# Router logits by another route: reads through (read weights times centred gate), in a fused memory-and-experts kernel, with routing 4 steps behind instead of 5

## What is computed

```python
x = x + attn(layernorm(x))       # out32 + (alpha * reads) @ W_read.T : a decaying memory, 4 heads of 64
x = x + ffn(layernorm(x))        # top 2 of 8 experts
# ffn:
logits = einsum('bsd,ed->bse', x, gate_w)
probs = softmax(logits); topk_probs, topk_idx = top_k(probs, 2)
h = gelu(x @ w1[e].T + b1[e]);  y = h @ w2[e].T + b2[e]
out = sum(y * topk_probs)
```

## Time and profile before

| | us |
|---|---|
| median of 3 timed runs | 559.88 (559.78, 559.88, 563.1) |
| the profiled execution | 562.67 |
| its span, first to last instruction | 560.9 |
| PE busy | 530.1 (95%) |
| DVE busy | 448.4 (80%) |
| ACT busy | 338.3 (60%) |
| POOL busy | 246.9 (44%) |

### The profile page before, as it was taken

How to read it: one execution, slowest core, us unless ns; L and a number is a source line. 1 busy time by engine, 2 the same in 40 slices (tenths; PEclk the granted TensorE clock), 3 DMA queues, 4 the chain that set the end, 5 groups by cost and what they waited for, 6 DMA issues and landing times.

```text
span 560.9 us, 17645 instructions
## 1 busy us (share of the span) xinstructions
PE 530.1 (95%) x5234; PEld 415.3 (74%) x5234; DVE 448.4 (80%) x1375; ACT 338.3 (60%) x856; POOL 246.9 (44%) x291
## 2 busy tenths in 40 slices
PE   7799899999999999999999999999999999999991
PEld 7677778778786777777777777777777777777770
DVE  4889999999987689868768787688777777778861
ACT  6899989898745876445545554455544544545540
POOL 5625778888746084523223233223322333322433
PEclk9999999999998999999999999999999999999997
DMA  5576867777345396433263364343344454344323
GB/s 161 201 229 225 258 185 234 210 222 231 126 105 129 87 216 101 71 60 62 51 103 56 53 105 77 63 68 61 61 63 79 78 78 75 68 64 67 63 37 36
DMA packets 85096, 63.33 MB, mean 113 GB/s; under 512 B 54224, under 2 KB 77392, under 8 KB 85008
## 3 DMA queue, kind: packets, MB, share of 16 engines
q1 hardware_dynamic: 71328, 43.94, 32.3%
q0 software_dynamic: 13392, 18.27, 17.3%
q10 hardware_dynamic: 288, 0.00, 0.0%
HBM read 37.56 MB, written 24.62 MB: 111 GB/s over the span
## 4 chain that ended last, share of the span: by engine, by line
PE 77%; DVE 10%; issue 4%; DMA 3%; ACT 2%; POOL 1%; SPq 1%; POOLq 0%; DVEq 0%; ACTq 0%
PE psum L1697 32%; PE psum L1712 21%; PE psum L1714 10%; PE psum L1509 3%; DVE weights L874 2%; PE psum L1592 2%; PE psum L1573 2%; PE psum L1599 2%; PE psum L1520 2%; DVE arena L1052 1%; PE psum L1559 1%; DMA arena<-sent_rows 1%; PE psum L1612 1%; PE psum L1496 1%; DVE arena L1063 1%
## 5 line engine op out<-in xcount | busy, mean ns | idle before, releaser
L1697 PE MATMUL psum<-arena,weights 128*128 128x256 f16 (+1 forms) x2208 | 279.7, 249 | 1.1 <-DVE arena L1316 1.0
L1697 PEld LDWEIGHTS psum<-arena,weights 128*128 x2208 | 187.4, 98 | 79.3 <-issue 4.1
L589 POOL DMA_INDIRECT out<-arena,tile_in x71 | 115.0, 1619 | 233.4 <-DVE arena L1343 126.9
L1712 PE MATMUL psum<-weights,arena 128*128 x556 | 211.7, 381 | 0.0
L826 ACT ACTIVATE arena<-psum,b_cur 128x256 f32<-128x256 f32 (+1 forms) x368 | 131.4, 423 | 129.9 <-PE psum L1697 115.6
L1714 PE MATMUL psum<-weights,arena 128*128 x556 | 152.0, 273 | 0.0
L1327 DVE TENSOR_TENSOR arena<-arena 128x512 f16<-128x512 f32 x142 | 98.5, 694 | 10.8 <-ACT arena L843 6.3
L559 POOL DMA_INDIRECT sent_rows<-arena,tiny x64 | 65.4, 1022 | 35.5 <-issue 17.8
L1323 DVE CAST arena<-arena 128x512 f16<-128x512 f32 x126 | 53.5, 424 | 8.8 <-ACT arena L826 8.5
L1712 PEld LDWEIGHTS psum<-weights,arena 128*128 128x128 f16 x556 | 54.4, 98 | 5.0
L1714 PEld LDWEIGHTS psum<-weights,arena 128*128 128x128 f16 x556 | 54.5, 98 | 4.6
(11 more groups left out here) (199 smaller groups left out, 642.9 us busy)
## 6 DMA issues: line engine op xcount, KB each, us to landing
weights<-in_experts SPq DMA_DIRECT2D x32, 512.0 KB, 4.8
arena<-sent_rows SPq DMA_DIRECT2D x100, 64.0 KB
arena<-in_b SPq DMA_DIRECT2D x46, 128.0 KB, 3.2
arena<-in_x SPq DMA_DIRECT2D x16, 256.0 KB, 3.4
out<-arena SPq DMA_DIRECT2D x16, 256.0 KB, 4.1
arena<-sent_rows SPq DMA_DIRECT2D x84, 32.0 KB
sent_rows<-pad SPq DMA_DIRECT2D x7, 265.0 KB, 4.6
tile_in<-sent_rows SPq DMA_DIRECT2D x71, 4.5 KB, 2.6
```

The lines of the kernel that those rows point to most:

```text
L589: pool.indirect_dma_start(out=out, out_offset=bass.IndirectOffsetOnAxis(ap=at_u, axis=0), in_=yout[:, u % 4], in_offset=None, compute_op=A ...
L1697: last = pe.matmul(ps_h[:, f % 2, mm * n:(mm + 1) * n], w1_of(e_of[i], k, lo, per * (f - GROUP[i]) + mm), turned[:, i % 2, part, k, 0:n], ...
L1712: pe.matmul(to, h_hi[:, z % 4, at], w2_of(e_of[t], m), start=(m == 0), stop=(m == MF - 1), skip_group_check=True)
```

## The change

Two layouts of the read weights are loaded, `wrT` (now with 8 more columns) and `wr_rows`. `mean_gate` and `centre_gate` take the mean off the gate, `gate_through_reads` and `read_gate` put Wr^T times the centred gate into the 8 new columns of `wrT`, so that `project` yields both projection and the reads' part of the logits, 264 columns over two PSUM banks. `gate_in_halves` splits the centred gate in F16. PE's `gate_x(n-3)` multiplies the halves of the normalised chunk, 12 F16 matmuls; ACT's `scale_gate` scales the result by POOL's `sides` (1 + root1); DVE's `logits`, now right after `residual`, adds the two parts. The scale rs2 goes into the exponential. `turn_normed`, `normed_transposed` and `score_experts` are gone. `LAG` is 4. ps_state and ps_gate_x share a PSUM bank, and so `gate_x`, `states`, DVE's `carry` and ACT's `scale_gate` wait for one another.

```diff
-LAG = 5
+LAG = 4
@@ sync: loads
             sp.dma_start(consts[:], const).then_inc(const_in, 16)
+            sp.dma_start(gateT[:], gate_w).then_inc(gate_in, 16)
...
-            sp.dma_start(wrT[:], w_read).then_inc(read_in, 16)
-            sp.dma_start(gateT[:], gate_w).then_inc(gate_in, 16)
+            sp.dma_start(wr_rows, w_read_rows).then_inc(rows_in, 16)
+            sp.dma_start(wrT[:, :, 0:D], w_read).then_inc(read_in, 16)
@@ gpsimd: step
+                if active(n, 0):
+                    reached(pool, "gate_x_done", n - 4)
+                    pool.tensor_tensor(roots[:], ve1, rs1[par], ALU.mult).then_inc(S["root_done"], 1)
+                    reached(pool, "root_done", n)
+                    pool.tensor_scalar(sides[:, n % 4], roots[:], 1.0 / WSCALE, 1.0 / WSCALE, ALU.mult,
+                                       ALU.add).then_inc(S["side_done"], 1)
-                if active(n, 5):
-                    m = n - 5
+                if active(n, 4):
+                    m = n - 4
@@ scalar
-            def normed_transposed(m):
+            def scale_gate(m):
+                reached(a, "gate_x_ps", m)
+                reached(a, "state_done", min(m, NCH - 2))
+                reached(a, "side_done", m)
+                reached(a, "logit_done", m - 1)
+                for b in range(B):
+                    last = a.activation(gate_x_part[:, b], ps_gate_x[:, b], ACT.Copy, scale=sides[:, m % 4, b:b + 1])
+                last.then_inc(S["gate_x_done"], 1)
@@ scalar: exponential
-                a.activation(shifted, shifted, ACT.Exp).then_inc(S["exp_done"], 1)
+                for b in range(B):
+                    last = a.activation(shifted[:, b], shifted[:, b], ACT.Exp, scale=rs2_of(m)[:, b:b + 1])
@@ scalar: step
-                if active(n, 5):
-                    exponential(n - 5)
+                if active(n, 3):
+                    scale_gate(n - 3)
+                if active(n, 4):
+                    exponential(n - 4)
...
-                if active(n, 4):
-                    normed_transposed(n - 4)
@@ vector: logits
-                reached(v, "logit_ps", m)
+                reached(v, "proj_ps", m)
+                reached(v, "gate_x_done", m)
-                v.tensor_copy(logit, ps_logit).then_inc(S["logit_done"], 1)
+                v.tensor_tensor(logit, ps_gate_read, gate_x_part[:], ALU.add).then_inc(S["logit_done"], 1)
@@ vector: carry
+                reached(v, "gate_x_ps", m)
@@ vector: before the first step
+            centre_gate()
             v.wait_ge(decay_masked, 4)
             weigh_scores(0)
             chunk_queries(1)
+            gate_in_halves()
             for j in splits(2):
                 split_low(j)
+            read_gate()
@@ vector: after last_step
-            place(m)
-            logits(m + 1)
-            largest(m + 1)
-            choose(m + 1)
+            largest(NCH - 1)
             split(2)
             prepare(1)
+            late_place(NCH - 2)
+            choose(NCH - 1)
             split(3)
-            late_place(m + 1)
             turn(2)
+            late_place(NCH - 1)
@@ tensor
+            def gate_through_reads():
+                pe.wait_ge(gate_centred, 1)
+                pe.wait_ge(rows_in, 16)
+                for k in range(KD):
+                    for j in range(KD):
+                        last = pe.matmul(ps_wr_gate[:, k], wr_rows[:, j, k * P:(k + 1) * P], gateT[:, j],
+                                         start=(j == 0), stop=(j == KD - 1))
+            def gate_x(m):
+                reached(pe, "gate_x_done", m - 1)
+                reached(pe, "state_done", m - 1)
+                reached(pe, "xlo_done", m)
...
+                for b in range(B):
+                    for at, (k, x, w) in enumerate(three):
+                        last = pe.matmul(ps_gate_x[:, b], xnT[:, x, s, b, k, 0:P], gate16[:, w, k],
+                                         start=(at == 0), stop=(at == len(three) - 1))
@@ tensor: rank
-                reached(pe, "x1_done", min(m + 2, NCH - 1))
+                reached(pe, "x1_done", min(m + 1, NCH - 1))
+                reached(pe, "logit_done", min(m + 1, NCH - 1))
@@ tensor: first pairs
             project(NCH - 1)
-            turn_normed(NCH - 2)
             pair(2, None)
-            rank(NCH - 3)
-            score_experts(NCH - 2)
+            rank(NCH - 2)
             pair(3, 0)
-            rank(NCH - 2)
+            rank(NCH - 1)
             pair(4, 1)
-            turn_normed(NCH - 1)
             pair(5, 2)
-            score_experts(NCH - 1)
             pair(6, 3)
-            rank(NCH - 1)
```

More of the change, by code:

```diff
@@ L141, in build @@
         wwT16 = ww16[:].rearrange("p h (k d) -> p h k d", k=KD)
-        wrT = sb("wrT", [P, KD, D])
+        wrT = sb("wrT", [P, KD, D + E])
         gateT = sb("gateT", [P, KD, E])
+        gate16 = sb("gate16", [P, 2, KD, E], F16)
+        gate_x_part = sb("gate_x_part", [P, B, E])
+        sides = sb("sides", [P, 4, B])
+        roots = sb("roots", [P, B])
+        rs2_slots = sb("rs2_slots", [P, 2, B])
+        rs2_of = lambda m: rs2_slots[:, m % 2]
         gam = sb("gam", [P, H])
@@ L232, in build @@
         moments2 = by_batch(small(B * 2))
-        ve2, rs2, shift2 = small(B), small(B), small(B)
+        ve2, shift2 = small(B), small(B)
         logit = by_batch(small(B * E))
@@ L578, in add @@
                 if i == 0:
-                    pool.wait_ge(x1_out[0], 16 * 6)
-                    pool.wait_ge(x1_out[1], 16 * 5)
+                    for s in range(2):
+                        pool.wait_ge(x1_out[s], 16 * len(range(s, NCH - LAG, 2)))
                 if i == NE:
@@ L593, in _ @@
             step(NCH + 2)
+            add(0)
             step(NCH + 3)
-            add(0)
-            step(NCH + 4)
             for i in range(1, NT):
@@ L672, in normalise @@
                 for b in range(B):
-                    last = a.activation(row[:, m % ROWS, b, 0:D], res_of(m)[:, b], ACT.Identity, scale=rs2[:, b:b + 1],
+                    last = a.activation(row[:, m % ROWS, b, 0:D], res_of(m)[:, b], ACT.Identity, scale=rs2_of(m)[:, b:b + 1],
                                         bias=shift2[:, b:b + 1])
@@ L1078, in step @@
                     moments(n)
-                if active(n, 5):
-                    choose(n - 5)
+                if active(n, 4):
+                    choose(n - 4)
                 if active(n, 1):
@@ L1086, in step @@
                     residual(n - 3)
+                    logits(n - 3)
                 for j in splits(n)[0:1]:
@@ L1096, in step @@
                     weigh_scores(n - 2)
-                if active(n, 5):
-                    place(n - 5)
                 if active(n, 4):
-                    logits(n - 4)
+                    place(n - 4)
                 if n == NCH:
@@ L1110, in last_step @@
                               zcol[:]).then_inc(S["xlo_done"], 1)
-                largest(NCH - 4)
+                largest(NCH - 3)
                 carry(NCH - 2)
-                choose(NCH - 4)
+                choose(NCH - 3)
                 weigh_scores(NCH - 1)
-                weigh_gates(NCH - 4)
+                weigh_gates(NCH - 3)
                 residual(NCH - 2)
+                logits(NCH - 2)
                 turn(0)
@@ L1119, in last_step @@
                 residual_moments(NCH - 2)
-                logits(NCH - 3)
                 low_tile(0)
-                largest(NCH - 3)
-                place(NCH - 4)
-                choose(NCH - 3)
+                largest(NCH - 2)
+                place(NCH - 3)
+                choose(NCH - 2)
                 prepare(0)
-                weigh_gates(NCH - 3)
                 turn(1)
@@ L1437, in _ @@
                     split(g)
-                if g == 5:
-                    logits(m + 2)
-                    largest(m + 2)
-                    choose(m + 2)
-                if g == 6:
-                    late_place(m + 2)
                 if g + 4 in STARTS:
@@ L1643, in _ @@
             keep_warm(16)
+            mean_gate()
             weigh(0)
@@ L1647, in _ @@
             states(0)
+            gate_through_reads()
             full_steps(step, 3)
-            turn_normed(NCH - 3)
+            gate_x(NCH - 2)
             values(NCH - 1)
@@ L1652, in _ @@
             project(NCH - 2)
-            score_experts(NCH - 3)
+            gate_x(NCH - 1)
             reads(NCH - 1)
-            rank(NCH - 4)
+            rank(NCH - 3)
             def w1_of(e, k, lo, m):
```

129 lines of the change are left out of this document (79 added, 50 removed).

## The result

The changed kernel takes 573.84 us (median of 4 runs, 569.74 to 575.91), the kernel before beside it 561.49: a ratio of 1.0205, interval 1.0127 to 1.0283. Two later sets of it gave 573.35 (1.0224) and 573.01 (1.0208). It is 2% slower; the prediction was 560.4 and no change, with a range up to 565.0.

The account below looks back on a forecast made before the run. DVE was taken to bound the three-piece steps, and a ring of waits through POOL most two-piece ones, with PE's ring to take over. Terms 1.2 + 0.2 + 1.6 - 2.5 = +0.5 on 559.88 gave 560.4 us, range 556.5 to 565.0.

Parts of the forecast that it names:

- these stand where it otherwise waits: nothing: ACT, every step: two added 8-column scalings and a second exponential fall into its waiting time and cost nothing.
- P: Ring of waits through POOL's last norm product, ACT and DVE: 9.74 a step before, forecast to stay near 9.76.
- Q: Ring of waits through PE's reads and turn_chunk, ACT and DVE: 9.28 a step before, forecast to become 9.87.
- steps of B: Eight two-piece steps from 74.15 to 151.53, no engine full: forecast 9.87 each for 9.67, +1.6 in all.
- first scatter starts at 7.94: POOL, every step: side ends at 7.77, scatters start at 7.94, norm chains follow at 12.89, 3.02 into the next step.
- step of A: Three-piece step between 22.75 and 74.15, bound by DVE's work at 10.43; the stretch was forecast +0.2.
- the rival on POOL: Later POOL chains make the second pow begin inside DVE's second piece: steps of 10.56, total 567.6; chance 0.10.
- The cover: POOL's margin: its second pow begins some 0.6 before DVE's second piece; chains 0.65 later would use it up.
- against: after 2.05 idle at 14.80 the clock stayed at 1.00: Argument against falls of PE's clock: one idle gap of 2.05 left the clock of the first stretches at 1.00.
- The forecast's rival: PE's new idle time in B and the passage drops its clock: three more falls, +4.5, 564.9; chance 0.08.
- The start: Stretch before chunk 2's chunk_low at 22.75: gate products and POOL's roots and sides make it +1.2 (0.6 to 1.9).
- The passage: Stretch from the last chunk's step into the experts: less PE work saves 2.5, with ends at -1.0 and -3.6.

Follow-up runs that it names:

- e2: The changed kernel without POOL's root and side from chunk 4 on (stale sides used instead): 569.42 us, ratio 1.0164.
- e6: The changed kernel, complete, with side computed on ACT from chunk 2 on and the scaling done in DVE's addition: 568.99 us, ratio 1.0137.
- e14: The changed kernel again, unaltered, as the base for a run with idle products: 573.01 us, ratio 1.0208.
- e1: The changed kernel with DVE's logits addition moved behind the first weight piece of the step: 575.43 us, ratio 1.0259.
- e11: The kernel before with only POOL's root and side added, their results unused: 575.35 us, ratio 1.0241.
- e5: The changed kernel with the logits addition behind DVE's first piece and no root and side on POOL from chunk 4 on: 565.92 us, ratio 1.0078.
- e13: The kernel before with PE's logit turns and gate products thinned, and the values' 12 products cut to 4, from chunk 2 on: 569.59 us, ratio 1.0150.
- e12: The changed kernel with idle PE products, 8 before the states and 12 before the reads, from the fourth step on: 575.07 us, ratio 1.0225.
- e15: The kernel of e16 with 5 idle PE products before the states and 6 before the reads, from the fourth step on: 563.03 us, ratio 1.0031.
- e16: The changed kernel, complete, with side on ACT from chunk 2 on and the logits addition behind DVE's first piece: 564.97 us, ratio 1.0064.
- e0: The changed kernel, unaltered, as the base of the first follow-up runs: 573.35 us, ratio 1.0224.
- e3: The changed kernel with 14 idle PE products before the reads from step 4 on: 574.06 us, ratio 1.0229.

## Why the prediction was wrong, point by point

The rings were the right picture, and three terms put on them were wrong.

*ACT, "these stand where it otherwise waits: nothing".* This step failed. ACT does wait 1.33 later in the step, but scale_gate stands early in it, behind a piece and the residual gain, and it is what DVE's addition waits for, 0.36 by starts. With the 0.09 of the addition itself, which the prediction had, DVE's pieces come 0.44 to 0.45 later, and both rings run over them: P 9.74 + 0.44 = 10.18, Q 9.28 + 0.32 + 0.45 = 10.05. Both sums were measured, the one in the changed kernel, the other in e2 and e6. Seven steps of B are longer by 0.44 (one by 0.66, where before had 9.52), 3.3 of its 4.9; the first step, 10.85 for 9.29, is the rest, and POOL's.

*POOL, "first scatter starts at 7.94", the next chain at 3.02.* Failed by two terms. A scatter follows the small operation side by 0.61, not by the 0.17 of the earlier trace rows. The trace of before has both: 0.17 behind an L551 that was held, and 0.61 in its one step of 9.52, where L551 escaped. That row was there to be read:

```profile
109.77 1.45 POOL L559 DMA_INDIRECT sent_rows<-arena,tiny  x1 [0.61 <-issue]
```

And a scatter that starts inside a piece is held itself (1.45 here, 1.56 in the step of A above, for 0.96); the sum had no term for that. In an even step the chain starts at 3.44 and the second pow at 5.79 (124.80), still 0.56 ahead of the second piece, which stands later too; so the rival on POOL stays away. It does so by very little. The fourth scatter starts 0.01 to 0.03 after the first piece (121.42 for 121.39, below) and takes 0.96. In e14, the same kernel, it starts 0.05 after the piece in the last step of A and takes 2.00; that step is 12.06, where the profiled execution had 10.87:

```profile
121.42 0.96 POOL L587 DMA_INDIRECT sent_rows<-arena,tiny  x1 [0.30 <-issue]
```
```profile
70.25 1.22 DVE L912 SCALAR_TENSOR_TENSOR weights<-weights 128x1024 f16<-128x1024 f32 x1
70.30 2.00 POOL L587 DMA_INDIRECT sent_rows<-arena,tiny  x1 [0.30 <-issue]
```

In the steps from 55.06 and 77.61 the first piece stands earlier (2.0 into the step, where the addition does not wait) and holds the fourth scatter, the chain starts at 4.13 in both, and the rival comes: 11.68 where A had 10.43, 10.85 where B had 9.29. That rival had its mechanism nearly right, the held operation being one earlier than its pow, and its size too (10.56 a step forecast, 10.84 in e1, 10.85 in e11); its chance of 0.10 was far too low. The cover was 0.65 for the start of the chain; the gap of 0.44 and the 0.6 of the held scatter, neither reckoned with, used it up. e11 shows that this alone makes the kernel before 13 us slower; e5 against e1, that it is worth 9.5 us in the changed kernel once the addition stands later.

*The clock, "against: after 2.05 idle at 14.80 the clock stayed at 1.00".* One gap behind a short stretch of work was no evidence for a gap in every step. The changed kernel's mean clock is 0.979 for 0.989. By e13 (2.9 us per 0.01) that is 3 us, by a straight line through the single runs of a set up to 4 (3.3 to 4.3 per 0.01 in ten of the sets; but 2.8 over all 16 runs of the changed kernel, 0.6 in e1 and nothing in e12, so this size is loose). The forecast's rival had said 4.5 for three more falls. That taking work from PE brings falls, and that they cost time, is shown by e13, whose rings are untouched; that it is so in the changed kernel too is argued from its lower clock, and e15 bears it out in the repaired one. The Trainium skill ("TensorE: Matmul & The Clock Gate", under the second failure mode of the clock) tells of an engine that idles briefly between groups of matmuls and swings between half and full clock; e13's trace agrees, 0.85 and 0.50 after gaps of 0.9.

Together: +6.8 in the profiled execution, whose clock was 0.987, the highest of its kernel; 2.3 to 3.4 for a mean clock 0.008 below that; and the profiled execution of before was itself 1.2 above its median. That is 10.3 to 11.4 of the 12.4 us. Some of the rest may be the last step of A, in which the profiled execution was lucky by 1.2 against e14's. Told by the runs instead: root and side off POOL give 3.9 back (e2), the later addition 3.5 more (e5), the few idle products 1.9 of what is left (e15 against e16), and e15 stands 1.9 above the kernel before.

*Terms that held, or nearly.* The twelve products 0.32, forecast 0.5 with 0.36 as an end. The start +0.9, forecast 1.2 (both executions without a fall there; e0's has one and comes at 23.73, e14's at 24.71). A's first step 10.17, forecast 9.87 without the addition's wait. The passage -1.5, forecast -2.5 with ends at -1.0 and -3.6; the wait ahead of rank(14) was to be over 2:

```profile
184.43 0.17 PE L1602 MATMUL psum<-late_mask,before 128*128 128x16 bf16 x1 [2.76 <-DVE tiny L1046]
```

The wait ahead of rank(15), forecast as well, does not show; the products of that place run at 1.2 GHz there (L1767 0.80 to 0.85 for 0.49), so PE came later. In e12's profile, at full clock there, it shows, 1.32 for the forecast 1.1:

```profile
191.75 0.18 PE L1602 MATMUL psum<-late_mask,before 128*128 128x16 bf16 x1 [1.32 <-DVE late_mask L946]
```

By the step lengths L573 ends 7.62 into a step, which the prediction had listed as a sign that it is wrong, beside a clock below 1.00 before 150 (the 0.97 of A).

*Not settled.* Why idle products gave 2 us in the repaired kernel (e15) and none in the changed one (e3, e12: there the clock rose, but the second stage was longer). And why the mean clock of e16 is still 0.984: PE idles 1.6 us of its step, but its profile has falls only at 12, 38 and 178.

## What to carry to other kernels

An engine that shows few waits may be full by gaps between its instructions: before you add an operation of 0.2 us to it, follow its whole train of a step by start times, gaps included, and ask which long operation of another engine it will run into. Cost a small operation by where its consumer stands, not by the idle time of its engine: ACT had 1.3 us to spare, at the wrong end of the step. Work taken from an engine that did not bound may cost through its clock.

## What the runs showed of the hardware

- A POOL operation of 0.2 us that starts while DVE runs a piece (scalar_tensor_tensor, 128x1024, two inputs) ends some 0.05 after that piece: 1.05 to 1.14 for 0.20. A scatter's issue that starts 0.05 or more inside one ends some 0.8 to 1.0 after it: up to 2.00 for 0.96. In all profiles together 30 start 0.01 to 0.03 inside, and none of these is held. One that starts within 0.1 ahead of the piece escapes, and the whole step goes by another ring (10.03 for 10.18). The Trainium skill ("GPSIMD Engine Reference", key points) says that GpSimd shares its SBUF interfaces with VectorE and that they contend when a VectorE instruction has two SBUF inputs; the holds agree.
- A scatter starts 0.61 after a small POOL operation that was not held, 0.17 after one that was held by a piece, and 0.30 after another scatter. These are the usual values in all 19 profiles where the gap is put down to no wait; 0.56 and 0.64 (unheld) and 0.28 (held) occur too.
- Twelve f16 products on 8 columns, with their weight loads, take 0.32: 0.027 each.
- Edits did not add: -4.0 and +2.1 alone, -7.4 together.
